# A decoder layer on one core: the value product of self-attention in three fp32r passes, with the work of GpSimd, ScalarE and SyncE reordered

## The reference, cut to what matters

```python
x = x + attn(layernorm(x))          # 32 query heads, 8 KV heads, head size 128, causal over 16 positions
x = x + xattn(layernorm(x), ctx)    # 16 heads, 4 components, mixed by "interference"
x = x + ffn(layernorm(x))           # one 1024 x 1024 matrix, built from factors
# in attn, for each KV group:
attn = jax.nn.softmax(scores, axis=-1)
out = jnp.einsum('bhst,bhtd->bhsd', attn, v)        # the value product
return jnp.einsum('sbe,he->sbh', out, weight_proj)
```

## Time and profile before

| | before |
|---|---|
| median of 3 runs | 3446.28 us |
| profiled execution | 3452.59 us |
| its span, first to last instruction | 3450.9 us |
| TensorE matmul busy | 3320.2 us, 96% |
| GpSimd busy | 1601.9 us, 46% |
| VectorE busy | 1470.4 us, 43% |
| ScalarE busy | 1199.3 us, 35% |
| mean granted TensorE clock | 0.98 |

### The profile page before, as it was taken

One profiled execution on the slowest core, in us unless ns is written; L12 is line 12 of the kernel. 1 busy time (PEld: TensorE's weight loads), 2 busy tenths in 40 slices (PEclk: granted clock), 3 DMA queues, 4 the chain that ended last, 5 costly groups with the idle time before them and its releaser, 6 DMA issues. The chain is left out here.

```text
span 3450.9 us, 47117 instructions
## 1 busy us (share of the span) xinstructions
PE 3320.2 (96%) x17332; PEld 2590.7 (75%) x17332; DVE 1470.4 (43%) x2359; ACT 1199.3 (35%) x2414; POOL 1601.9 (46%) x1015
## 2 busy tenths in 40 slices
PE   6999999999999999999999869999999999989999
PEld 5777777777777777877777657777777777763587
DVE  3232242322342223332322336666665666652353
ACT  3223232232332323332222235554554555540110
POOL 3767667576775767754343323333433333320000
PEclk9999999999999999999999989999999999988999
DMA  4333344333434333343232067777677677633141
GB/s 158 118 116 115 118 138 141 116 115 118 137 102 155 116 118 113 128 159 97 73 109 73 31 244 217 221 228 233 197 217 243 208 208 222 204 114 147 37 146 74
DMA packets 165327, 502.54 MB, mean 146 GB/s; under 512 B 20400, under 2 KB 20528, under 8 KB 165176
## 3 DMA queue, kind: packets, MB, share of 16 engines
q1 hardware_dynamic: 162872, 492.06, 45.0%
q10 hardware_dynamic: 2304, 8.39, 0.6%
HBM read 416.48 MB, written 83.89 MB: 145 GB/s over the span
## 5 line engine op out<-in xcount | busy, mean ns | idle before, releaser
L53 PE MATMUL sa_u<-sa_ln_xh,sa_wh 128*128 128x512 f32 x1536 | 628.3, 409 | 4.1 <-DVE sa_ln_xl L258 4.1
L54 PE MATMUL sa_u<-sa_ln_xl,sa_wh 128*128 128x512 f32 x1536 | 599.7, 390 | 0.0
L55 PE MATMUL sa_u<-sa_ln_xh,sa_wl 128*128 128x512 f32 x1536 | 599.3, 390 | 0.0
L455 POOL TENSOR_TENSOR sa_wl<-sa_wraw,sa_wh 128x1024 fp32r<-128x1024 f32 x192 | 460.5, 2403 | 276.3 <-ACT sa_wh L628 276.3
L498 POOL TENSOR_TENSOR sa_pl<-sa_praw,sa_ph 128x1024 fp32r<-128x1024 f32 x128 | 318.3, 2521 | 448.4 <-ACT sa_ph L671 448.4
L1070 POOL TENSOR_TENSOR ca_probs<-ca_probs,ca_inv 128x512 f32<-128x512 f32 x256 | 267.2, 1053 | 555.3 <-DVE ca_inv L1437 555.2
L53 PE MATMUL sa_pr<-sa_ph,sa_oh 128*128 128x512 f32 x1024 | 428.5, 418 | 0.1
L758 DVE TENSOR_TENSOR sa_ol<-sa_o,sa_oh 128x512 fp32r<-128x512 f32 x128 | 88.5, 692 | 741.2 <-ACT sa_oh L683 741.2
L54 PE MATMUL sa_pr<-sa_pl,sa_oh 128*128 128x512 f32 x1024 | 400.5, 391 | 0.0
L55 PE MATMUL sa_pr<-sa_ph,sa_ol 128*128 128x512 f32 x1024 | 400.1, 391 | 0.0
L766 DVE TENSOR_TENSOR sa_acc<-sa_pr,sa_acc 128x512 f32<-128x512 f32 x256 | 176.5, 691 | 508.0 <-PE sa_pr L55 507.7
(11 more groups left out here) (183 smaller groups left out, 5651.7 us busy)
## 6 DMA issues: line engine op xcount, KB each, us to landing
sa_wraw<-in_wqkv SPq DMA_DIRECT2D x192, 512.0 KB, 3.6
sa_praw<-in_wproj SPq DMA_DIRECT2D x128, 512.0 KB, 3.6
ca_wh<-w_folded_hi SPq DMA_DIRECT2D x96, 512.0 KB, 5.1
ca_wl<-w_folded_lo SPq DMA_DIRECT2D x96, 512.0 KB, 6.6
ca_kstack<-k_parts SPq DMA_DIRECT2D x192, 128.0 KB, 3.4
ca_qstack<-q_parts SPq DMA_DIRECT2D x96, 256.0 KB, 5.6
ca_owraw<-in_wo SPq DMA_DIRECT2D x32, 512.0 KB, 3.7
sa_raw<-in_w_turned SPq DMA_DIRECT2D x24, 512.0 KB, 6.3
```

The costliest lines, as they stand in the source:

```text
L53: nc.tensor.matmul(out, ah, bh, start=(first and i == 0), stop=False)
L54: nc.tensor.matmul(out, ah, bl, start=False, stop=False)
L55: ins = nc.tensor.matmul(out, al, bh, start=False, stop=(last and i == len(parts) - 1))
L455: nc.gpsimd.tensor_tensor(wl[:, u % 3], wraw[:, u % 3], f32(wh[:, u % 3]), ALU.subtract).then_inc(w_split, 1)
```

## The change

In the self phase the value product becomes three fp32r passes, with v and the spread probabilities each in a high and a low part. v's high part is ScalarE's copy, its low part a new subtraction on VectorE (`low_v`). VectorE transposes all probabilities by one instruction into `probsT` (the buffer of `masked`); ScalarE spreads them into `diagh` in four copies of 32 partitions (`spread_probs`, behind its third output weight and its first unit copy); GpSimd subtracts four times into `diagl` (`low_probs`). Between two of these subtractions GpSimd waits for the former one's completion. GpSimd's order becomes: three terms of the mixing, `low_probs`, `weights(n, 3)`, the four `pl`, and the rest as before. SyncE loads wraw 4 and 5 of a group in that group's own step, behind `raw`, so that the stores of the folded parts no longer come behind them.

In the cross phase SyncE issues the third weights ahead of the last store of a closed block; three of the four reloads of `acc` move into the next step, behind the key stores; each tile of the next block's x is loaded at the end of its own step (steps 1 to 4) instead of two at the start of steps 1 and 2. There and in the feed-forward part some semaphores are merged into others with counts adjusted (left out below): waits on `v_set` and `kstack_zeroed` become waits on `cleared`, `delta_ready` is counted in `u_scaled`, `biases_summed` in `s_steps`.

```diff
--- before.py
+++ after.py
@@ -329,11 +329,14 @@
         kT = sb("sa_kT", [P, 2, BT])
         qT = sb("sa_qT", [P, 2, QPG, BT])
         vT = sb("sa_vT", [P, BT])
-        v = sb("sa_v", [P, 2, TILES, HD])
+        vh = sb("sa_vh", [P, 2, TILES, HD], F32R)
+        vl = sb("sa_vl", [P, 2, TILES, HD], F32R)
         BLK = TILES * QPG
         masked = sb("sa_masked", [P, BLK, QW])
         probs = sb("sa_probs", [P, BLK, QW])
-        diag = sb("sa_diag", [P, BLK, QUADS, QW])
+        probsT = masked
+        diagh = sb("sa_diagh", [P, BLK, QUADS, QW], F32R)
+        diagl = sb("sa_diagl", [P, BLK, QUADS, QW], F32R)
...
         s_done = sem("sa_s_done")
         s_masked = sem("sa_s_masked")
         s_shifted = sem("sa_s_shifted")
         exp_done = sem("sa_exp_done")
         soft_steps = sem("sa_soft_steps")
-        TURNED, TOPPED, SUMMED, INVERTED, SCALED = range(1, 6)
+        TURNED, TOPPED, SUMMED, INVERTED, SCALED, SPREAD = range(1, 7)
+        diag_hi = sem("sa_diag_hi")
         diag_ready = sem("sa_diag_ready")
         diag_zeroed = sem("sa_diag_zeroed")
...
@@ -410,6 +415,9 @@
                 if s.steady:
                     sp.wait_ge(mix_steps, s.m * MIXES + MIXES)
                     sp.dma_start(raw[:], tile_of(w_turned, s.m)).then_inc(raw_loaded, 16)
+                if s.proj and s.attn:
+                    for u in range(4, U):
+                        weights(s.g, s.n, u)
                 if s.proj:
 
                     for h in range(QPG):
@@ -419,7 +427,7 @@
                     sp.wait_ge(ln.turned, s.b * ln.GROUPS + ln.GROUPS)
                     load_x(s.b + 1)
                 if s.nxt:
-                    for u in range(U):
+                    for u in range(4):
                         weights(s.next_g, s.n + 1, u)
                 if s.steady:
                     sp.wait_ge(fold_split, s.m + 1)
@@ -447,7 +455,8 @@
             pool.sem_inc(w_split, 3)
             pool.sem_inc(p_split, QPG)
             pool.sem_inc(mix_steps, MIXES)
-            nc.gpsimd.memset(diag[:], 0.0).then_inc(diag_zeroed, 1)
+            nc.gpsimd.memset(f32(diagh[:]), 0.0).then_inc(diag_zeroed, 1)
+            nc.gpsimd.memset(f32(diagl[:]), 0.0).then_inc(diag_zeroed, 1)
 
             def weights(n, u):
 
@@ -492,14 +501,37 @@
                 nc.gpsimd.tensor_tensor(foldl[:], mixed, f32(foldh[:]), ALU.subtract).then_inc(fold_split, 1)
 
             def step(s):
-                if s.attn:
-                    for h in range(QPG):
+                def out_weights(hs):
+                    if not s.attn:
+                        return
+                    for h in hs:
                         pool.wait_ge(p_hi, s.m * QPG + (h + 1))
                         nc.gpsimd.tensor_tensor(pl[:, h], praw[:, h], f32(ph[:, h]), ALU.subtract
                                                 ).then_inc(p_split, 1)
+
+                def low_probs():
+
+                    if not s.attn:
+                        return
+                    pool.wait_ge(diag_zeroed, 2)
+                    pool.wait_ge(w_split, s.n * U + (6 if s.proj else 3))
+                    if s.steady:
+                        pool.wait_ge(mix_steps, s.m * MIXES + (MIXES + 5))
+                    for q in range(QUADS):
+                        rows = slice(q * QW, (q + 1) * QW)
+                        pool.wait_ge(diag_hi, s.m * QUADS + (q + 1))
+                        if q > 0:
+                            pool.wait_ge(diag_ready, s.m * QUADS + q)
+                        nc.gpsimd.tensor_tensor(diagl[rows, :, q], probsT[rows], f32(diagh[rows, :, q]), ALU.subtract
+                                                ).then_inc(diag_ready, 1)
+                    pool.wait_ge(diag_ready, s.m * QUADS + QUADS)
+
+                mix_rows(s, 0, [0, 1, 2])
+                low_probs()
                 if s.proj:
                     weights(s.n, 3)
-                    mix_rows(s, 0, [0, 1, 2])
+                out_weights(range(QPG))
+                if s.proj:
                     weights(s.n, 4)
                     mix_rows(s, 0, [3])
                     mix_rows(s, 1, [0, 1])
@@ -574,8 +606,9 @@
                         pe.wait_ge(diag_ready, m * QUADS + QUADS)
                     pe.wait_ge(o_split, m * TILES + (t + 1))
                     heads = slice(t * QPG, (t + 1) * QPG)
-                    nc.tensor.matmul(o_ps[t % 2][:], v[:, mp, t], diag[:, heads].rearrange("p h q n -> p (h q n)"),
-                                     start=True, stop=True).then_inc(o_done, 1)
+                    three_passes(nc, o_ps[t % 2][:],
+                                 [(vh[:, mp, t], vl[:, mp, t], diagh[:, heads].rearrange("p h q n -> p (h q n)"),
+                                   diagl[:, heads].rearrange("p h q n -> p (h q n)"))]).then_inc(o_done, 1)
 
                 def project(t):
                     if not s.attn:
@@ -652,8 +685,8 @@
                     if not s.proj:
                         return
                     act.wait_ge(v_turned, n + 1)
-                    nc.scalar.activation(v[:, s.par].rearrange("p t d -> p (t d)"), v_ps[:], ACT.Copy
-                                         ).then_inc(v_copied, 1)
+                    nc.scalar.activation(vh[:, s.par].rearrange("p t d -> p (t d)"), v_ps[:], ACT.Copy
+                                         ).then_inc(v_hi, 1)
 
                 def high_fold():
                     if not s.steady:
@@ -682,10 +715,23 @@
                     act.wait_ge(o_done, m * TILES + (t + 2))
                     nc.scalar.activation(oh[:, t % 2], o_ps[t % 2][:], ACT.Copy).then_inc(o_hi, 1)
 
+                def spread_probs():
+
+                    if not s.attn:
+                        return
+                    act.wait_ge(diag_zeroed, 2)
+                    act.wait_ge(o_done, m * TILES + 1)
+                    act.wait_ge(soft_steps, m * SPREAD + SPREAD)
+                    for q in range(QUADS):
+                        rows = slice(q * QW, (q + 1) * QW)
+                        nc.scalar.activation(diagh[rows, :, q], probsT[rows], ACT.Copy).then_inc(diag_hi, 1)
+
                 exps()
                 out_weights([0, 1])
                 copy_unit(0)
-                out_weights([2, 3])
+                out_weights([2])
+                spread_probs()
+                out_weights([3])
                 copy_unit(1)
                 copy_unit(2)
                 copy_v()
@@ -721,12 +767,21 @@
             def step(s):
                 m = s.m
 
+                def low_v():
+                    if not s.proj:
+                        return
+                    dve.wait_ge(v_hi, s.n + 1)
+                    nc.vector.tensor_tensor(vl[:, s.par].rearrange("p t d -> p (t d)"), v_ps[:],
+                                            f32(vh[:, s.par]).rearrange("p t d -> p (t d)"), ALU.subtract
+                                            ).then_inc(v_copied, 1)
+
                 if not s.attn:
+                    low_v()
                     return
 
                 def softmax():
                     i = m + 1
-                    done = m * 5
+                    done = m * SPREAD
                     dve.wait_ge(s_done, i)
                     nc.vector.tensor_tensor(masked[:], s_ps[:].rearrange("p (k n) -> p k n", k=BLK),
                                             causal_t[:].unsqueeze(1).broadcast_to([P, BLK, QW]), ALU.add
@@ -747,11 +802,8 @@
                     nc.vector.tensor_tensor(probs[:], probs[:], inv[:].unsqueeze(2).broadcast_to([P, BLK, QW]),
                                             ALU.mult).then_inc(soft_steps, 1)
                     dve.wait_ge(soft_steps, done + SCALED)
-                    dve.wait_ge(diag_zeroed, 1)
-                    dve.wait_ge(o_done, m * TILES + 1)
-                    for q in range(QUADS):
-                        rows = slice(q * QW, (q + 1) * QW)
-                        nc.vector.transpose(diag[rows, :, q], probs[rows]).then_inc(diag_ready, 1)
+                    nc.vector.transpose(probsT[:].rearrange("p k n -> p (k n)"),
+                                        probs[:].rearrange("p k n -> p (k n)")).then_inc(soft_steps, 1)
 
                 def low_o(t):
                     dve.wait_ge(o_hi, m * TILES + (t + 1))
@@ -989,15 +1041,12 @@
 
             for s in STEPS:
                 after_closing = s.n > CH and s.g == 1
+                if s.attn and s.proj:
+                    next_weights(STEPS[s.m], 2)
                 if after_closing:
                     store_x2(STEPS[s.m], TILES - 1)
-                if s.attn and s.proj:
-                    next_weights(STEPS[s.m], 2)
                 if s.more:
                     load_context(s.b + 1, s.g)
-                    if s.g in (1, 2):
-                        sp.wait_ge(ln.turned, s.b * ln.GROUPS + ln.GROUPS)
-                        load(s.b + 1, ln.x, ln.loaded, [2 * s.g - 2, 2 * s.g - 1])
                 if not s.attn:
                     sp.wait_ge(c_split, KC)
```

(17 more changed lines are left out.)

17 lines of the change are left out of this document (7 added, 10 removed).

## The result

The changed kernel takes 3557.77 us (median of 4 runs, 3549.88 to 3576.86), the kernel before, run beside it, 3445.43 (3443.0 to 3452.0). The ratio is 1.0331 with a 95% interval of 1.0286 to 1.0376: 112 us slower, where 126 were forecast.

The account below looks back on a forecast made before the run. TensorE, busy 96% of the span, was taken as the bound; -22 (product) + 95 (stall) + 8 (last step) + 53 (clock) - 8 (cross part) = +126 on 3446 gave 3572 us, range 3475 to 3630.

Parts of the forecast that it names:

- shorter products: Value product on TensorE: three fp32r matmuls instead of one fp32 save 0.17 us on each of 128 products, 22 us.
- four low parts on POOL: GpSimd's spread subtractions in each attention step: four of 1.27 us plus waits of 0.17, 5.8 us.
- stall at `project(0)`: TensorE waits 3.1 us for four pl before the first output projection, in 31 full steps: 95 us.
- clock behind it: Granted clock falls after each stall, costing 0 to 3.4 us a step; middle 1.7 times 31: 53 us.
- last attention step: No projection units hide the spread and low parts there, so the four pl end later: +8 us once.
- cross part: Cross phase, SyncE reordered: the 6.1 us ca_wl waits go, perhaps a third of 19.7 for scores; -8 us (-20 to +5).
- the 2.4 that the prediction gave as a sign: Lower end of the sign that a self-phase attention step gets longer by 2.4 to 5.8 us.
- T0: Start of an attention step's scores on TensorE, from which the forecast counts times; 623.64 in the profiled step before.
- Rivals 1 and 5: Rival 1: low parts cheap, no stall, 3420 us, 12%; rival 5: stall under 1 us, within 10 us of before, 4%.
- the upper end: GpSimd subtraction on 32 partitions taken at 1.27 us, as for 128, rather than a quarter, 0.32.
- Rival 2: Stall at project(0) without any fall of the granted clock: 3519 us, 28%.
- rival 3: Granted clock falls for 6.8 us at nearly each stall: 3624 us, 10%.

Follow-up runs that it names:

- interleaved: Changed kernel with GpSimd order pl(0), weights(3), low parts, pl(1) to pl(3), weights(4), mixing; high_fold behind high_o(3); SyncE's self order as before: 3440.83 us, 0.9984.
- warm: Changed kernel with 11 unused matmuls added on TensorE ahead of the wait in project(0): 3534.10 us, 1.0255 of the kernel before.
- cross_only: Self phase of the kernel before with the cross and feed-forward phases of the changed one: 3432.71 us, 0.9958.
- order_only: Changed kernel's GpSimd order (mixing, weights(3), four pl), SyncE order and cross part, but the fp32 value product of before: 3426.24 us, 0.9939.
- pl01_first: Changed kernel with GpSimd doing output weights 0 and 1 ahead of the spread's low parts: 3462.26 us, 1.0046 of the kernel before.
- self_only: Changed kernel with SyncE's old order in the cross phase, merged semaphores kept: 3568.13 us, 1.0366 of the kernel before.
- no_waits: Changed kernel without GpSimd's three waits between the four low-part subtractions: 3535.51 us, 1.0263 of the kernel before.

## Why the prediction was right, step by step

| step | predicted | measured |
|---|---|---|
| shorter products | -22 | a step without a gap in `interleaved` is 59.06 for 59.77: -22 |
| four low parts on POOL | 5.8 us | 5.57 |
| stall at `project(0)` | 3.1 us x 31 = 95 | 2.85 x 31 = 88 |
| clock behind it | 53 (0 to 105) | 29 by the lengths of the steps, 24 by `warm` |
| last attention step | +8 | +9.5, of which 8.0 in its two gaps |
| block borders, beside the rows above | nothing | about +12 |
| cross part | -8 | -14 (`cross_only`) |
| sum | +126 | +102 by these parts, +97 by the two traces, +112 by the medians |

- **Product and stall** were right, and rest on the queue argument: not that POOL works more (it has idle time in every step), but what stands behind the new work until PE asks for it. `order_only` and `pl01_first` show it from both sides. The low parts with the wait behind them took 5.73 us for 5.8. The stall is 0.25 us shorter than predicted by small things: the weight and the four `pl` took 11.75 us and not 11.85, PE came 0.03 later, and 0.07 is rounding in the forecast's own sum. A step without a fall of the clock is 2.2 us longer than before, a little under the 2.4 that the prediction gave as a sign. The chain itself came as forecast: scaling 0.69 instead of 2.94, spread start at T0 + 9.2 (9.2 = 663.14 - 653.96) for 9.2, low parts from T0 + 9.9 to T0 + 15.4 for 15.7. Rivals 1 and 5 fall with it.
- **A part of the partitions costs as much as all.** 32x512 takes 1284 ns on POOL, have 1274 for 128x512. The choice of the upper end was the one that decided, and it was right.
- **The clock** is the term that was mis-sized. The step of the prediction was that a stall of 3 us lies between the rows of 3.44 and 2.48 and costs 1.7 us in each of 31 steps. The clock fell at 15 of the 31, for 3.4 or 6.8 us: some 29 us, 0.9 us a step on average. Rival 2 (no fall, 3519) is 39 us below the result and rival 3 (6.8 us each, 3624) 66 above; `warm` shows that the clock's part is real. That the middle between two rows came within a factor of two is in part luck, for the length of the stall did not decide: stalls of 2.81 to 2.86 us stand in all three groups. The row of 3.44 was no measure of its own length either: in the trace of before, the fall begins at 559.9, in the middle of this idle time, and another one of 2.46 us ends at 558.10, just ahead of it.
- **The last step** came as forecast in its gaps. Before, and after:

```profile
1968.13 3.75 PE L577 MATMUL sa_o<-sa_diag,sa_v 128*128 128x512 f32 x4 [10.58 <-issue]
```
```profile
2079.43 0.76 PE L53 MATMUL sa_o<-sa_diagh,sa_vh 128*128 128x512 f32 x1 [12.71 <-issue]
...
2088.72 0.79 PE L53 MATMUL sa_pr<-sa_ph,sa_oh 128*128 128x512 f32 x1 [6.40 <-POOL sa_pl L509]
```

From start to start the gaps are 12.98 us ahead of the product and 7.03 ahead of the projection, where before they were 10.85 and 1.13: +8.0. The step is 9.5 us longer. The prediction had no clock here: the projection now starts in a stretch at 0.50 that lasts until 2094.7, where before the clock was back at 1.00 from 1973.0 on, 1.0 us behind the projection's start.
- **The block borders** were left out. I had followed SyncE's queue for `wraw`, not for the loads of x behind `praw` in the last step of a block. VectorE's wait for them in after:

```profile
481.26 0.69 DVE L214 BATCH_NORM_STATS2 sa_ln_stats<-sa_ln_x 128x6 f32<-128x512 f32 x1 [12.19 <-DMA sa_ln_x<-in_x_rows]
```

PE then waits for `sa_acc`, 7.9 us in three waits, and for `weights(3)` and the low parts, 3.0 and 2.0 in two waits each; against this, PE's waits for scores (`sa_s`) fell from 11.7 to 5.7 us. That makes 7 us. The 8 border steps are 39.5 us longer, of which 17 are their stalls and shorter products and 10 the clock at `project(0)` (estimates from the ordinary steps), so 12 are left: these 7, and lower clock at the borders.

- **The cross part** gained more than I gave it: besides the 6.1 us for `ca_wl`, some 5 of the 19.7 for scores, where a third had been forecast. In after's own trace the cross phase is 19 us shorter, in `cross_only` 16; the medians give 14. Both traces have 51 us at 0.50 in it, where before has 75, worth up to 12 us: the forecast had no term for the clock here.

The parts that belong to the self phase (-22, 88, 29, 9.5, 12) make +116.5; the trace of after has +118.6 there and the medians of `self_only` +121. The trace is of the fastest run of after, and the median lies 8 us above it, with more low clock in two of the slower runs (0.969 and 0.966 on average over the span for 0.973).

**Open.** Why the scores at the turn of a block wait between 2 and 5 us in different kernels was not tried. Which of the stalls the clock falls at is not shown, nor can its share be told more closely than 24 to 34 us.

## What to carry to other kernels

When work is added to a helper engine that has idle time, its share of busy time says nothing: write down its queue from the added work to the next result that the bounding engine asks for, and place the new work behind what is ready earlier. Then follow the delay through the DMA queue whose loads wait for that engine's buffers, and look at the steps that differ from the steady ones (block borders, the last step). A short stall repeated in every step also costs clock; with PE as the bound, the 0.17 us saved on each of 128 products (22 us) were worth a quarter of one misplaced wait of 3 us in each of 31 steps (88 us).

## What the runs showed of the hardware

- GpSimd's subtraction costs the same on 32 partitions (1284 ns for 32x512) as on 128 (1274 ns), and four in a row on different quarters without any wait between them take 5.36 us, with waits 5.57: no overlap, and 0.07 us for each wait.
- Of 31 stalls, 28 of them 2.6 to 2.9 us long, the granted clock fell to 0.50 at 15 and stayed at 16. A fall that began inside the stall lasted 6.8 us and made the step 2.8 us longer (four cases, the price read from two ordinary steps), one that began behind it 3.4 us and 1.6. In `no_waits`, with stalls and steps shorter by 0.2 us, there were 14 stretches for 20. Filling the stall with matmuls of no use gave back 24 us.
- A subtraction on VectorE with both inputs in SBUF takes 0.69 us with POOL idle, and 2.8 beside POOL's subtractions, which lengthen too, from 9.40 to 11.24 us for four.
- At the granted clock of 0.50 an fp32r matmul of 128x512 follows the last after 0.43 us (2079.99 to 2080.42), at 1.00 after 0.23.
